# The order of the steps on VectorE, ScalarE, SP and GpSimd in a two-layer adapter kernel

## The chip, the cores and the metric

The kernel runs on one core of a Trainium2 chip. The metric is the device time of one execution in microseconds (us). All matrix products run on TensorE; the other engines (VectorE, ScalarE, GpSimd) and the DMA queue that SyncE (SP) issues have their own instruction streams and meet only at semaphores.

## The reference

Two layers of the same form follow each other. Each of 128 items has a role out of three (its row of weights), and the roles drawn are only two of them, so a layer sorted by role has one change of weights in it.

```python
h = einsum('bsh,bhk->bsk', x, W_down[role]) + b_down[role]     # x: (128, 128, 1024), K = 512
h = gelu(h, approximate=False)
u = einsum('bsk,bkh->bsh', h, W_up[role]) + b_up[role]
y = x + u
x = (y - mean(y)) * rsqrt(var(y) + 1e-5) * gamma[role] + beta[role]
```

## The kernel before

**Pairs and steps.** The items are sorted by role and taken two at a time: 65 pairs in a layer, 130 pairs `p` in all (layer 0 is pairs 0 to 64, layer 1 is 65 to 129). `e` is 0 or 1, the item within a pair. Every engine runs one function `step(i)` (or `begin(i)` and `end(i)`) for a rising pair number `i`, and works in it on several pairs at once: `i` goes down, `w = i-2` is split for the up product, `u = i-3` goes up and is added to its rows, `u-1 = i-4` (for GpSimd and SP `z`) is normalised and stored. In layer 1 the rows come from `mid`, where layer 0 stored them.

**TensorE.** Matrices are multiplied as three products of high and low parts (high x high, high x low, low x high) in full-width matmuls of 512 columns. A step i has 90 of them, in blocks of six: `product(u, 0)`, `down(i, 0, 0)`, `product(u, 1)`, `down(i, 0, 1)`, `product(u, 2)`, `down(i, 0, 2)`, `product(u, 3)`, `down(i, 0, 3)`, `product(u, 4)`, `down(i, 1, 0)`, `product(u, 5)`, `down(i, 1, 1)`, `product(u, 6)`, `down(i, 1, 2)`, `down(i, 1, 3)`. The up product is done by a scheme of seven products instead of eight (Winograd's form), whose sums of blocks of h are made by GpSimd (`sums`) and whose sums of weights by VectorE (`factors`). Steps 0 to 2 have no products, steps 130 to 132 have no `down`. The products 0, 2, 4, 6 go to the bank `bX`, the products 1, 3, 5 to `bZ`, where some stay to be added to. Product 2 waits for `onto` 1 to have read its bank, product 3 for `onto` 2, product 4 for `onto` 3, product 5 for `last_onto` 4, product 6 for `last_onto` 5 (all by the count `s_v`).

**What TensorE waits for besides.** `down(i, 0, 0)` needs `xl`, the low part of x (VectorE's `low_x(i, 0)`, after ScalarE's `high_x(i, 0)`), the bias in its bank (`seed_d`), and an increase of `s_wd[0]` by VectorE's `ready(i, s_wd[0])`, which comes in every step whether weights are new or not. `s_wd[1]` stands before `down(i, 0, 2)`. The products wait in the same way for `s_wu[0]` (products 0 and 1), `s_wu[1]` (2 and 3) and `s_wu[2]` (4 to 6), and for `low_h` 0 to 3, the low parts of h and its sums: product 0 for the first, products 1 and 2 for the second, product 3 for the third, product 5 for the fourth.

**VectorE** runs `end(i-1)` and then `begin(i)` as one body. Its `low_*` and `take_*` functions subtract high parts; `transpose_h` and, in layer 1, `transpose_x` transpose what DMAs laid out in blocks; `onto` and `last_onto` add a bank to the rows (the evictions; the last of them also sum the row), `mean`, `variance` and `scale` (rows minus mean, times gamma) belong to the normalisation. **ScalarE** rounds to the high parts (`high_*`, `take_*`), does `gelu`, writes biases into banks (`seed_*`), squares and `normal` (times 1/sigma), and issues the loads of new weights (`load_up`, `load_down`, 2 MB each). **GpSimd** does `sums`, two small steps of `norm` and `shift` (plus beta), and increases `s_cg`, for which `scale` waits. **SP** issues all other DMAs: `store_h` writes gelu's result to `htok` in DRAM, `load_h` fetches it back in blocks once it has landed, `load_blocks` fetches x in blocks (`xq`, for the down product), `load_rows` fetches x in rows, `store` writes rows out.

**Order and queues.** The order within a step is written out by hand, and each engine takes its instructions in that order. `kinds.when_new(p, do)` is an `If` on a register: it runs `do` only where pair p has other weights than the pair before. That is so for pairs 30, 65 and 95, so that new down weights are taken for steps 30, 65 and 95, and their new up weights are first used in steps 33, 68 and 98 (`w` is such a pair in steps 32, 67 and 97). `when_far` runs loads and `factors` for the same pairs; `when_near` never finds a pair here.

**Loops.** `steps` and `plain_steps` unroll six steps into the body of a hardware loop. VectorE's jumps back lie between `begin` and the following `end`, in layer 0 before `end(9)`, `end(15)` and so on (steps 10, 16, ... 58 of TensorE), in layer 1 before `end(74)`, ... `end(122)` (steps 75, 81, ... 123):

```python
def body(i):
    end(i + -1)
    begin(i)
```

## Time and profile before

| | us |
|---|---|
| median of 3 runs | 2741.23 (2740.98 to 2743.66) |
| profiled execution, its own time | 2742.87 |
| its span, first to last instruction | 2741.1 |
| TensorE busy | 2682.4 (98%) |
| VectorE busy | 2200.2 (80%) |
| ScalarE busy | 1668.7 (61%) |
| GpSimd busy | 1375.2 (50%) |

PE is TensorE, PEld its weight loads, DVE VectorE, ACT ScalarE, POOL GpSimd, SP SyncE; an engine with a q is its queue, which issues DMAs and increases semaphores. The busy time of an engine is the union of its rows; matmul rows overlap. In a timeline a row is the start in us from the span's start, its length in us, the engine, the source line, the operation, what it writes and reads, how many alike were merged, and in brackets how long the engine stood idle before it and what ended that. L537 is a matmul of `down`, L549 of `product`, L888 `low_wd`, L907 `low_wu`, L913 to L917 `factors`, L926 the last step of `take_wu_0`, L959 `ready`, L968 `transpose_x`, L975 `low_x`, L982 `transpose_h`, L997 `low_h`, L1007 `onto`, L1015 `last_onto`, L1023 `mean`, L1038 `scale`, L661 `high_x`; L287 is the load of up weights, L334 `load_blocks` in layer 1, L381 `store_h`, L389 `load_h`, L311 the load of up biases.

### The profile page before, as it was taken

To read this page: it belongs to the slowest core of one execution; us is meant where nothing else is said; L and a number is where in the kernel's file an instruction comes from. 1 tells how busy PE (TensorE), PEld (TensorE's weight loads), DVE (VectorE), ACT (ScalarE), POOL (GpSimd) and SP (SyncE) were. 2 spreads that over 40 slices of the span, in tenths; PEclk is the share of its full clock that TensorE was granted. 3 is DMA by queue.
4 is the path that set the end of the run, shared out by engine and by line. 5 is a ranking of instruction groups with operands and counts; after the bars stand their busy time and mean duration, and the time that the engine had idled before them with its cause. 6 is when DMAs were issued, how large, how long until landed. Compare 5 with 4: busy or idle time off the path is not lost.

```text
span 2741.1 us, 54380 instructions
## 1 busy us (share of the span) xinstructions
PE 2682.4 (98%) x11720; PEld 2200.6 (80%) x11720; DVE 2200.2 (80%) x3360; ACT 1668.7 (61%) x2906; POOL 1375.2 (50%) x1050
## 2 busy tenths in 40 slices
PE   8999999998999999999989999999989999999996
PEld 6888888887888888888778888888768888888885
DVE  6777777779777777777898888888888888888886
ACT  5656656666656665666656665665656565665664
POOL 1455455555545555555444454554445455545545
PEclk9999999999999999999999999999999999999999
DMA  6656566566666656656766566666766666666664
GB/s 221 219 198 219 200 209 211 202 233 223 222 205 204 209 205 209 212 201 225 235 200 220 187 222 203 206 214 201 242 197 214 199 223 191 222 204 203 214 193 149
DMA packets 360737, 573.36 MB, mean 209 GB/s; under 512 B 40162, under 2 KB 239970, under 8 KB 359394
## 3 DMA queue, kind: packets, MB, share of 16 engines
q1 hardware_dynamic: 358850, 554.14, 61.5%
q10 hardware_dynamic: 1440, 15.47, 1.6%
q14 instruction: 435, 3.56, 0.4%
q8 instruction: 12, 0.20, 0.0%
HBM read 364.97 MB, written 204.47 MB: 208 GB/s over the span
## 4 chain that ended last, share of the span: by engine, by line
PE 87%; DVE 6%; issue 5%; ACT 1%; DMA 1%; POOL 1%; DVEq 1%; ACTq 0%; POOLq 0%; SPq 0%
PE pD L537 46%; PE bX L549 23%; PE bZ L549 18%; DVE wul L907 1%; DVE xt L1015 1%; DVE hl L997 1%; DVE xT L968 0%; DVE xt L1007 0%; DMA rwu<-in_Wu 0%; DVE xt L1038 0%; DVE hT L982 0%; DVE xl L975 0%; DVE wdl L888 0%; POOL cs L486 0%; POOL cs L488 0%
## 5 line engine op out<-in xcount | busy, mean ns | idle before, releaser
L537 PE MATMUL pD<-wdh,xh 128*128 128x512 f32 x2080 | 811.6, 390 | 13.7 <-DVEq L959 10.1
L478 POOL TENSOR_TENSOR xt<-xt,cgb 128x1024 f32<-128x1024 f32 x258 | 630.1, 2443 | 364.8 <-ACT xt L729 364.8
L537 PE MATMUL pD<-wdh,xl 128*128 128x512 f32 x2080 | 810.4, 390 | 0.0
L537 PE MATMUL pD<-wdl,xh 128*128 128x512 f32 x2080 | 810.1, 389 | 0.0
L486 POOL TENSOR_TENSOR cs<-hT 128x256 f32<-128x256 f32 x130 | 150.7, 1159 | 910.6 <-DVE hT L982 910.6
L721 ACT ACTIVATE pC<-xt,nmean 128x512 f32<-128x512 f32 x520 | 359.8, 692 | 257.7 <-DVE nmean L1023 248.9
L729 ACT ACTIVATE xt<-xt,rstd 128x1024 f32<-128x1024 f32 x258 | 297.1, 1152 | 307.4 <-POOL rstd L471 303.9
L537 PEld LDWEIGHTS pD<-wdh,xh 128*128 128x128 f32 x2080 | 391.0, 188 | 100.3 <-DVEq L959 13.3
L537 PEld LDWEIGHTS pD<-wdh,xl 128*128 128x128 f32 x2080 | 391.0, 188 | 81.6
L537 PEld LDWEIGHTS pD<-wdl,xh 128*128 128x128 f32 x2080 | 391.1, 188 | 80.8
L549 PE MATMUL bX<-wuh,hh 128*128 128x512 f32 x1040 | 406.8, 391 | 18.2 <-DVE xt L1007 10.5
L549 PE MATMUL bX<-wul,hh 128*128 128x512 f32 x1040 | 405.1, 390 | 0.0
L549 PE MATMUL bX<-wuh,hl 128*128 128x512 f32 x1040 | 405.0, 389 | 0.0
L997 DVE TENSOR_TENSOR hl<-cs,hh 128x512 fp32r<-128x512 f32 x260 | 302.0, 1180 | 112.1 <-issue 105.7
L711 ACT ACTIVATE hh<-cs 128x512 fp32r<-128x512 f32 x260 | 163.9, 630 | 359.4 <-PE bX L549 240.5
L1038 DVE SCALAR_TENSOR_TENSOR xt<-xt,nmean,cgb 128x1024 f32<-128x1024 f32 x260 | 327.3, 1299 | 10.3 <-POOLq L499 6.7
L549 PE MATMUL bZ<-wuh,hh 128*128 128x512 f32 x780 | 307.4, 394 | 13.3 <-issue 7.6
L549 PE MATMUL bZ<-wul,hh 128*128 128x512 f32 x780 | 304.9, 391 | 0.0
L549 PE MATMUL bZ<-wuh,hl 128*128 128x512 f32 x780 | 304.8, 391 | 0.0
L1007 DVE TENSOR_TENSOR xt<-bX,xt 128x512 f32<-128x512 f32 x260 | 178.7, 687 | 129.8 <-PE bX L549 129.0
L549 PEld LDWEIGHTS bX<-wuh,hh 128*128 128x128 f32 x1040 | 195.3, 188 | 65.4 <-DVE xt L1007 15.0
L1015 DVE SCALAR_TENSOR_TENSOR xt<-bX,xt 128x512 f32<-128x512 f32 x260 | 177.1, 681 | 88.1 <-PE bX L549 88.0
(119 smaller groups left out, 3830.5 us busy)
## 6 DMA issues: line engine op xcount, KB each, us to landing
xq<-in_xB SPq DMA_DIRECT2D x130, 512.0 KB, 3.6
htok<-hg SPq DMA_DIRECT2D x260, 256.0 KB, 2.9
hq<-htok SPq DMA_DIRECT2D x1040, 64.0 KB, 2.2
xt<-in_x SPq DMA_DIRECT2D x130, 512.0 KB, 4.2
mid<-xt SPq DMA_DIRECT2D x130, 512.0 KB, 3.7
xq<-mid SPq DMA_DIRECT2D x520, 128.0 KB, 3.1
xt<-mid SPq DMA_DIRECT2D x130, 512.0 KB, 4.6
out<-xt SPq DMA_DIRECT2D x128, 512.0 KB, 3.0
```

What stands on the lines that cost most here:

```text
L478: eng.tensor_tensor(xt[:, k, :], xt[:, k, :], cgb[:, 1, :], ALU.add).then_inc(s_o, 1)
L486: eng.tensor_tensor(cs[:, 0, :], b1, b2, ALU.add).then_inc(s_S, 1)
L537: last = eng.matmul(pD[e][:, :], a[:, e, 128 * k:128 * k + 128], w[:, k, :], start=False, stop=(k == 7 and n == 2), skip_group_check=True)
L549: last = eng.matmul(bank[:, :], a[:, left, 128 * c:128 * c + 128], w[:, n, c, :], start=(start and c == 0 and m == 0), stop=(c == 1 and m ...
L711: eng.activation(dst, src, ACT.Copy).then_inc(s_hh, 1)
L721: eng.activation(junk[:, :], xt[:, u.slot(e), K * m:K * m + K], ACT.Square, bias=nmean[:, n:n + 1], accum_out=ssq[:, b, m, e:e + 1]).then_ ...
L729: eng.activation(xt[:, k, :], xt[:, k, :], ACT.Copy, scale=rstd[:, n:n + 1]).then_inc(s_z, 1)
L907: eng.tensor_tensor(wul[:, n, :, :], block, wuh[:, n, :, :].bitcast(fp32), ALU.subtract)\
L997: eng.tensor_tensor(blocks, src, high.bitcast(fp32), ALU.subtract).then_inc(s_hl, 1)
L1007: eng.tensor_tensor(half(u, e, m), bank[:, :], half(u, e, m), ALU.add).then_inc(s_v, 1)
L1015: eng.scalar_tensor_tensor(out=half(u, e, m), in0=bank[:, :], scalar=1.0, in1=half(u, e, m), op0=ALU.mult, op1=ALU.add, accum_out=ys[:, b, ...
L1038: eng.scalar_tensor_tensor(out=xt[:, k, :], in0=xt[:, k, :], scalar=nmean[:, n:n + 1], in1=cgb[:, 0, :], op0=ALU.add, op1=ALU.mult).then_i ...
```

## The change

Steps are put in another order on four engines, and nothing else is changed: no instruction is added or removed, and every wait stays with its step. On VectorE the evictions and the later parts of a step change places with the work on new weights (`take_*`, `factors`), one of the two `scale` goes behind `last_onto` 4, `low_h` 0 goes behind it too, `transpose_x(i+1, 1)` and `last_onto` 7 go to the head of `end`, and `ready(i+1, s_wd[0])` stands behind them. On ScalarE `gelu(i, 0)` goes ahead of `high_x(i+1, 0)`, `high_h` 0 ahead of `gelu(i-1, 1)`, and the loads of weights are spread over `end`. On SP `load_blocks(i+1, 1)` goes behind `load_h(v, 1)`, both stores go ahead of `store_h(i, 0)` and `load_blocks(i+2, 0)`, and the loads of biases and gains go from the end into the middle. On GpSimd `sums` goes behind the increase of `s_cg` and the wait for new gains.

```diff
--- before.py
+++ after.py
@@ -411,21 +411,21 @@
                 kinds.read(i + 1)
                 load_h(v, 0)
                 store_h(v, 1)
+                load_rows(w, 0)
+                load_h(v, 1)
                 if not (i + 1).first():
                     load_blocks(i + 1, 1)
-                load_h(v, 1)
-                load_rows(w, 0)
-                load_rows(w, 1)
-                store(z, 0)
-                store_h(i, 0)
-                if not (i + 1).first():
-                    load_blocks(i + 2, 0)
-                store(z, 1)
-                kinds.when_new(u, gains)
                 if i.first():
                     up_biases(i)
                 if not v.first():
                     kinds.when_new(v, up_biases)
+                kinds.when_new(u, gains)
+                load_rows(w, 1)
+                store(z, 0)
+                store(z, 1)
+                store_h(i, 0)
+                if not (i + 1).first():
+                    load_blocks(i + 2, 0)
 
             steps(eng, step, -1, NPH + 4, 2, 6, 5)
             for k in range(4):
@@ -492,11 +492,11 @@
 
             def step(i):
                 w, z = i + -2, i + -4
-                sums(w)
                 if z.exists():
                     kinds.read(z)
                     kinds.when_new(z, take_gb)
                     eng.sem_inc(s_cg, 1)
+                sums(w)
                 norm(z)
                 shift(z, 0)
                 shift(z, 1)
@@ -747,49 +747,49 @@
                 kinds.read(i + 2)
                 if not i.first():
                     high_x(i, 1)
-                gelu(i + -1, 1)
-                if not i.first():
-                    seed_d(i, 1)
                 if (i + -2).first():
                     take_wu_2(Pair(0))
-                high_h(i + -2, 0)
                 if i.first():
                     fetch_up(eng, adapter(i), 0)
                 if not (i + -3).first():
                     kinds.when_new(i + -3, take_wu_2)
+                high_h(i + -2, 0)
+                gelu(i + -1, 1)
+                if not i.first():
+                    seed_d(i, 1)
 
             def end(i):
                 u, w = i + -3, i + -2
                 if not (i + 1).first():
                     kinds.when_new(i + 1, load_bias)
+                high_h(w, 1)
                 kinds.when_near(w, load_up)
+                normal(u + -1, 0)
                 kinds.when_far(i, load_up)
+                gelu(i, 0)
                 kinds.when_near(i + 1, load_down)
-                kinds.when_far(i + 2, load_down)
-                high_h(w, 1)
                 if not w.first():
                     kinds.when_new(w, take_wu_0)
-                normal(u + -1, 0)
                 if not (i + 1).first():
                     high_x(i + 1, 0)
-                gelu(i, 0)
-                high_h(w, 2)
+                if (i + -1).first():
+                    take_wu_0(Pair(0))
+                kinds.when_far(i + 2, load_down)
+                seed_x(w)
+                normal(u + -1, 1)
                 if not (i + 1).first():
                     seed_d(i + 1, 0)
-                normal(u + -1, 1)
                 if not (i + 1).first():
                     kinds.when_new(i + 1, take_wd_0)
-                seed_x(w)
+                high_h(w, 2)
+                square(u, 0, 0)
                 seed_z(w)
-                square(u, 0, 0)
+                high_h(w, 3)
                 square(u, 0, 1)
-                high_h(w, 3)
+                square(u, 1, 0)
                 if not (i + 1).first():
                     kinds.when_new(i + 1, take_wd_1)
-                square(u, 1, 0)
                 square(u, 1, 1)
-                if (i + -1).first():
-                    take_wu_0(Pair(0))
 
             steps(eng, halves(begin, end), -1, NPH + 5, 0, 5, 5)
 
@@ -1072,44 +1072,44 @@
                     last_rows(u + -1)
                     return
                 onto(u, 1, X, 0, 0)
+                transpose_h(w, 0)
                 if not i.first():
                     kinds.when_new(i, take_wd_1)
-                ready(i, s_wd[1])
                 if u.first():
                     take_wu_6(Pair(0))
-                transpose_h(w, 0)
+                ready(i, s_wd[1])
                 transpose_h(w, 1)
+                onto(u, 2, bZ, 1, 1)
+                if u.last():
+                    variance(u + -1)
                 if not i.first():
                     low_x(i, 1)
+                onto(u, 3, X, 0, 1)
                 if (i + -1).first():
                     factors(Pair(0))
                 if (i + -2).first():
                     take_wu_1(Pair(0))
+                if not u.last():
+                    variance(u + -1)
                 kinds.read(i + 1)
-                onto(u, 2, bZ, 1, 1)
-                low_h(w, 0)
-                if u.last():
-                    variance(u + -1)
-                onto(u, 3, X, 0, 1)
                 if not u.first():
                     kinds.when_new(u, take_wu_2)
                 ready(u, s_wu[2])
+                scale(u + -1, 0)
+                last_onto(u, 4, bZ, 0, 1, 3)
                 kinds.when_near(w, factors)
-                if not u.last():
-                    variance(u + -1)
+                low_h(w, 0)
                 if only_up(i):
                     low_h(w, 1)
-                scale(u + -1, 0)
                 scale(u + -1, 1)
-                last_onto(u, 4, bZ, 0, 1, 3)
                 transpose_x(i + 1, 0)
                 last_onto(u, 5, X, 1, 1, 2)
                 if not w.first():
                     kinds.when_new(w, take_wu_0)
                     ready(w, s_cb)
-                ready(w, s_wu[0])
                 if not (i + 1).first():
                     low_x(i + 1, 0)
+                ready(w, s_wu[0])
                 last_onto(u, 6, bZ, 0, 0, 1)
                 mean(u, 0, 6)
 
@@ -1117,21 +1117,20 @@
                 u, w = i + -3, i + -2
                 if (u + -1).last():
                     return
+                transpose_x(i + 1, 1)
+                last_onto(u, 7, bX[u.c % 2], 1, 0, None)
                 if not (i + 1).first():
                     kinds.when_new(i + 1, take_wd_0)
                 ready(i + 1, s_wd[0])
-
-                if not only_up(i):
-                    low_h(w, 1)
-                transpose_x(i + 1, 1)
-                low_h(w, 2)
                 if w.first():
                     take_wu_4(Pair(0))
-                last_onto(u, 7, bX[u.c % 2], 1, 0, None)
-                mean(u, 1, 7)
                 kinds.when_far(i + -1, factors)
                 if not w.first():
                     kinds.when_new(w, take_wu_1)
+                if not only_up(i):
+                    low_h(w, 1)
+                mean(u, 1, 7)
+                low_h(w, 2)
                 ready(w, s_wu[1])
                 low_h(w, 3)
                 if (i + -1).first():
```

## Rows read from the trace of the kernel before

**Rows 1.** The page, part 1: busy us (share) xinstructions of each engine

```profile
PE 2682.4 (98%) x11720; PEld 2200.6 (80%) x11720; DVE 2200.2 (80%) x3360; ACT 1668.7 (61%) x2906; POOL 1375.2 (50%) x1050
```

**Rows 2.** The chain of waits: start us, us, what; 26 such pieces, first two

```profile
70.33 2.72 PE pD L537 x12
...
90.73 2.72 PE pD L537 x12
```

**Rows 3.** TensorE by stretches: us, busy (matmuls), granted clock, DMA share, GB/s

```profile
590.00:720.00 130.00, 121.25 (x523) 0.99 0.67 223
...
1930.00:2070.00 140.00, 128.03 (x542) 0.99 0.71 224
...
2690.00:2741.10 51.10, 30.44 (x119) 0.90 0.39 140
```

**Rows 4.** Timeline of TensorE, step 75

```profile
1547.06 0.39 PE L549 MATMUL bX<-wuh,hh 128*128 128x512 f32 x1
...
1555.30 0.50 PE L549 MATMUL bZ<-wuh,hh 128*128 128x512 f32 x1
...
1567.71 0.39 PE L549 MATMUL bX<-wuh,hh 128*128 128x512 f32 x1
```

**Rows 5.** Timeline of VectorE around two jumps of its loop

```profile
318.57 1.30 DVE L997 TENSOR_TENSOR hl<-cs,hh 128x512 fp32r<-128x512 f32 x2 [5.17 <-issue]
...
1542.55 0.21 DVE L1023 TENSOR_SCALAR nmean<-ys 128x1 f32<-128x1 f32 x1
...
1547.22 0.69 DVE L997 TENSOR_TENSOR hl<-cs,hh 128x512 fp32r<-128x512 f32 x1 [4.45 <-issue]
...
1549.58 0.67 DVE L1015 SCALAR_TENSOR_TENSOR xt<-bX,xt 128x512 f32<-128x512 f32 x1
```

**Rows 6.** Timeline of ScalarE, step 74

```profile
1538.73 1.03 ACT L661 ACTIVATE xh<-xT 128x1024 fp32r<-128x1024 f32 x1 [0.57 <-DVE xT L968]
```

**Rows 7.** Timelines of VectorE and TensorE at the first layer's new up weights

```profile
645.97 1.22 DVE L913 TENSOR_TENSOR rwu<-rwu 128x1024 f32<-128x1024 f32 x1
...
660.18 4.57 DVE L907 TENSOR_TENSOR wul<-rwu,wuh 128x1024 fp32r<-128x1024 f32 x2
...
664.67 3.42 DVE L926 TENSOR_TENSOR rwu<-twu,rwu 128x1024 f32<-128x1024 f32 x1
...
670.23 0.50 PE L537 MATMUL pD<-wdh,xh 128*128 128x512 f32 x1 [2.31 <-DVEq L959]
...
676.85 0.50 PE L549 MATMUL bX<-wuh,hh 128*128 128x512 f32 x1 [2.22 <-DVE xt L1007]
...
680.56 2.90 DVE L907 TENSOR_TENSOR wul<-rwu,wuh 128x1024 fp32r<-128x1024 f32 x2
...
685.43 0.47 PE L549 MATMUL bX<-wuh,hh 128*128 128x512 f32 x1 [2.64 <-DVEq L959]
```

**Rows 8.** Timeline of TensorE at the last new down weights

```profile
1968.74 0.50 PE L549 MATMUL bZ<-wuh,hh 128*128 128x512 f32 x1 [1.61 <-DVE xt L1007]
```

**Rows 9.** Timelines of VectorE and TensorE in step 131

```profile
2710.73 2.47 DVE L1038 SCALAR_TENSOR_TENSOR xt<-xt,nmean,cgb 128x1024 f32<-128x1024 f32 x2
...
2713.91 0.75 PE L549 MATMUL bZ<-wuh,hh 128*128 128x512 f32 x1 [3.17 <-issue]
```

**Rows 10.** Timelines of ScalarE's, SP's queues and VectorE, step 95

```profile
1968.13 0.35 ACTq L287 DMA_DIRECT2D rwu<-in_Wu  x1
...
1969.04 2.33 SPq L334 DMA_DIRECT2D xq<-mid  x4
...
1976.81 1.74 SPq L389 DMA_DIRECT2D hq<-htok  x4
...
1979.03 1.26 DVE L968 STREAM_TRANSPOSE xT<-xq 128x1024 f32<-128x1024 f32 x1 [0.50 <-DMA xq<-mid]
```

**Rows 11.** Timelines of SP and ScalarE near the start

```profile
27.50 0.34 SPq L311 DMA_DIRECT2D cbu<-in_bu  x1
...
35.44 1.06 ACT L661 ACTIVATE xh<-xq 128x1024 fp32r<-128x1024 f32 x1 [7.04 <-DMA xq<-in_xB]
```


## The prediction

> **What bounds the kernel now.** I read the page first. TensorE is busy for 98% of the span [rows 1], so every other engine counts only where TensorE waits for it. The chain of waits then gives the pace: the same twelve matmuls come back every 20.40 us [rows 2], one step of 90 matmuls, 0.227 us each. 11,700 matmuls at that pace are 2652 us of the 2741.1 us span. The other 89 us are what an order of steps can touch: a start of some 13 us before the first real matmul, some 11 us after the last, and about 65 us of pauses. Third, TensorE by stretches [rows 3] shows where these are: 8.8 us idle at the change of weights in the first layer, 12.0 at the change in the second, and 20.7 in the last 51 us; the second layer's first weights have their share too. A pause costs some 0.16 us more than its idle time, because a matmul's row is 0.39 long and the pace 0.227, and more where the clock dips (0.90 at the end [rows 3]). The ordinary steps are at the floor: there an earlier operation gains nothing, and only a later one can matter.
>
> **Where the limits lie within a step.** Count from the first matmul of product 0. `down(i,0,0)` starts at 1.36, product 1 at 2.72, product 2 at 5.44, product 3 at 8.16, product 5 at 13.6, product 6 at 16.3 (blocks of six matmuls, 1.36 each). Product n's bank is readable some 0.15 us after its end, so `last_onto` 7 can start at 17.85.
>
> **Ordinary steps.** Walking the new order through with the durations of rows, VectorE's `scale`, 1.24 us each [rows 9], now has one copy before `last_onto` 4 and one after, with `low_h` 0 (0.4) between them. `ready(s_wd[0])`, which releases `down(i+1,0,0)`, is moved from before `low_h` 1 to behind `transpose_x(i+1,1)` and `last_onto` 7. In an ordinary step of layer 1 that is about 18.75, against 21.76 when it is wanted; `low_h` 1 ends near 19.6, wanted at 23.1. ScalarE's `high_h` 2 goes from 13.5 to about 17, and its use is at 28. SP stores both halves before `store_h(i,0)`: it goes from 14.8 to about 19.5, and what it feeds is used a step later. All hidden: cost 0, with 2 to 3 us of cover. If the cover were gone the price would be that of the next part.
>
> **The jump at the end of VectorE's loop body.** VectorE's code is a loop of six steps, and at each jump it stands still: 4.45 us [rows 5], with no releaser but "issue", always right after `mean(u,0)` and before the first operation of `end` (5.17 in the longest, in layer 0). In layer 1 `mean` starts at 15.9 of the step before (1542.55 less 1526.66), so the first operation runs at 1547.22, and TensorE's step began at 1547.06 [rows 4]. `ready` is now the first thing after the jump, just in time. In the new order it stands behind a 1.25 us transposition and `last_onto` 7 (0.69).
> There is also a delay ahead of the jump. In layer 1 `transpose_x(i+1,0)` now comes after `low_h` 0 and a second `scale`: it ends near 13.4 instead of 12.0. ScalarE's `high_x`, which waits for it already [rows 6], ends at 14.6; `low_x` and `last_onto` 6 follow, and `mean` starts near 16.5, 0.6 later. Then 4.4 for the jump, 1.16 and 0.69: `ready` at 22.9 to 23.1 against 21.76, so TensorE pauses for 1.2 us, with the restart 1.35. From this the kernel before has its own loss at these steps to be taken off: product 3 starts late there (1555.30) and the step is 20.65 long, 0.25 too much [rows 4]; eight such steps have lost 1.7 in all. The new order has `onto` 2 ahead of `low_x(i,1)` and ends that. Eight jumps: 8 x 1.35 - 1.7 = **+9.1**. Bounds: 0.9 each if the skipped `If`, now behind the jump's cover, saves 0.25 (+5.5), and 1.8 each if the wait grows (+12.7).
> In layer 0 there is no transposition, and `mean` is not later. `ready` comes 0.8 after the jump ends; it passes if the jump ends before 0.5 of the step. It ended at 0.88 in the worst [rows 5], so one or two pauses: **+0.5** (0 to 2).
> The Trainium skill ("Runtime: NRT & Kernel Launch", Instruction fetch mechanics) says that a taken branch to code outside the fetched window stalls until it is fetched. The trace agrees at the loop's jump (4.45 us), while skipped `If` blocks cost 0.25 to 0.5. If the rule struck the skipped blocks too, the new places of the `If`s right behind the jump would be worse than I count.
>
> **New up weights (three times).** Now VectorE runs `take_wu_0` (4.57 for two `wul`, 3.42 for `b11` [rows 7], stretched because GpSimd runs at the same time) ahead of `low_x`, and TensorE waits 2.31; then `take_wu_1` makes `onto` 1 late, 2.22; then `take_wu_2` with product 4, 2.64. In the new order: `factors` (three at 1.22) ahead of `low_h` 1 makes product 1 late by 0.4 in the step before; `last_onto` 4, `scale` and the others are earlier, so `ready(s_wd[0])` is about 0.4 late in layer 0 and 1.7 in layer 1 (two transpositions more); `take_wu_1`, now ahead of `low_h` 1, delays product 1 by 1.9 to 2.2; `take_wu_2` ahead of `scale` and `last_onto` 4 still holds product 4 back, by 1.9 to 2.0. So 5.0 for 7.2 in layer 0, and 6.1 for about 8.4 in layer 1.
> **New down weights (three times).** `take_wd_1` and `low_x(i,1)` stood before `onto` 2, and product 3 waited 1.61 [rows 8]; with `onto` 2 ahead of `low_x` (1.2) some 0.3 to 0.5 is left. That is 1.3 less in layer 0, 2.1 at the layer's start and 3.6 at the last change.
> **Blocks behind a load of weights.** This goes against the change. SP's `load_blocks(i+1,1)` moves behind `load_h(v,1)` and `load_rows`, and VectorE's `transpose_x(i+1,1)` moves ahead of `last_onto` 7. At the last change the 2 MB of up weights were issued at 1968.13, the blocks at 1969.04, and the transposition found them only at 1979.03, 10.9 after the weights' issue; nothing urgent stood behind it [rows 10]. Now `last_onto` 7 and `ready` do: blocks at 22.5, `ready` at 24.5, a pause of 2.7 us, at both layer-1 loads. Once, in step 94, SP's own loop jump and the load of down weights coincide; blocks near 22, then `take_wd_0`, `ready` at 26.4, a pause of 4.6. The landing of `htok`, for which `load_h(v,1)` waits, took 8 us there (1968.48 to 1976.81 by the second of these issues). Together 10 us, bounds 0 (blocks issued before the weights) and 14.
> Sums with the restarts: layer 0 **-4.5**; the layer's start -5.5 + 3.0 = **-2.5**; the last change, before it 17.8 of pauses, after it 0.5 + 6.1 with restarts (8.4), a jump 1.35, blocks 3.0 and 4.6: **0**.
>
> **The end.** In the last steps, without `down`, product 5 waits for `last_onto` 4, which stands behind two `scale` (2.47 together) and these behind GpSimd's `sums`, because `s_cg` is increased after `sums`: 3.17 of pause [rows 9], and much the same a step earlier. Now `s_cg` is first, and one `scale` is behind. I get product 5 earlier by 3.3, 4.4 and 4.4 in the three steps, but part is lost again, because `low_h` 2 waits for GpSimd's `shift`: last matmul earlier by **-4** (-1 to -6).
> **The start.** `gelu(0,0)` (0.58) goes ahead of `high_x(1,0)`, and `cbu`'s load, now at 27.50, is issued before the blocks for which ScalarE waited 7.04 us [rows 11]; `ready(s_wd[1])` follows a transposition: **+1** (0 to +3).
> GpSimd's `take_gb` ahead of `sums`, `gains` ahead of `load_rows(w,1)`: both are hidden, by some 2 us, three times; if not, up to +3.
>
> **Sum:** -4.5 - 2.5 + 0 - 4 + 1 + 9.1 + 0.5 = -1.4 to the profiled execution (2742.87, with 1.8 around its span). The median is 2741.23; half a microsecond of the small unknowns above is kept for a loss: 2740.3.
>
> **Rivals.**
> A, the sum: gains at the weights and the end, eaten by the loop jumps. Chance 0.43. 2735.8 to 2746.7.
> B, the gains win: blocks land in time (10 less) or the jump's pauses are 0.9 (3.6 less). For it: SP's issues at the first change of layer 1 came close to the transposition's time anyway (the wait was only 0.50). Against it: the order is fixed and the transposition's place moves forward by itself. 2727 to 2735, 2730 if blocks alone are in time. Chance 0.33.
> C, slower: blocks are late not only near weights. In the step behind each SP loop jump I get the blocks' landing at 19.3 and the transposition from 19.5, `ready` at 21.45 against 21.76. It decides from a landing after 19.7: each microsecond is paid eight times, so 1 us late is +8, 2749; with the longer jump pauses 2752. Chance 0.24.
> D, nothing moves: VectorE would have to run 1.3 us ahead at the jumps and stay as late at weights. It is within A's band; the rows with 4.45 speak against it.
> The skill's page "SBUF — State Buffer" (Who interferes with whom) has the lock between VectorE and GpSimd held for a whole instruction. `b11`, 3.42 long in place of 1.22, agrees; moved operations may meet GpSimd elsewhere, which would be spread over B and C.
>
> **Numbers.** A measurement here tells 0.2%, 5.5 us, from no change. Faster 0.33, same 0.43, slower 0.24. The range reaches into B and C, 2729 to 2750; A's own is 2736 to 2746.
>
> **What would show it.** After VectorE's jump in layer 1: transposition, `last_onto` 7, and TensorE paused by 1.0 to 1.5 us before `down(i,0,0)`, released by `ready`; steps of 21.7 there. Product 3 never late at jumps. Pauses at product 1, no longer at `onto` 1, at new up weights. In steps 66 and 96 the transposition waiting for the blocks. Last matmul 4 us sooner. It is wrong if `mean(u,0)` isn't later in layer 1, if blocks land before 16.7, or if ordinary steps aren't 20.40.

## The result, and the profile after

| | before | after |
|---|---|---|
| median of 19 runs each | 2742.59 (2740.98 to 2746.26) | 2747.16 (2743.09 to 2755.03) |
| ratio, 95% interval | | 1.0016 [1.0010, 1.0023] |
| profiled execution, its span | 2742.87, 2741.1 | 2747.39, 2745.5 |

The change costs some 4.6 us. That is inside the band of 0.2% and inside the range (2729 to 2750), but the forecast had its sign the other way (2740.3, 0.9 under the 2741.23 that it started from). The page, part 1, and TensorE by stretches (us, busy with matmuls, granted clock, DMA share, GB/s), which answer to [rows 1, 3]:

```profile
PE 2684.8 (98%) x11720; PEld 2202.1 (80%) x11720; DVE 2158.2 (79%) x3360; ACT 1680.4 (61%) x2906; POOL 1318.5 (48%) x1050
```

```profile
590.00:720.00 130.00, 126.11 (x539) 0.97 0.65 220
1930.00:2070.00 140.00, 127.04 (x537) 0.95 0.65 210
2690.00:2745.50 55.50, 35.22 (x142) 0.92 0.39 143
```

The first stretch has gained, the second has lost, and the ordinary pace of 20.40 is unchanged. To see every pause, each gap from one matmul's start to the next is taken, less the pace of 0.2267 us, and summed by stretch. All kernels run later stand in the same table, since it is what tells them apart ("start" is up to 80 us, "first" 600 to 720, "layer 1" 1310 to 1445, "last" 1925 to 2125, "end" from 2660; "rest" is the ordinary steps and the jumps; "jumps" is the length of the steps behind VectorE's jumps in layer 1, without the one in the last change of weights). All in us:

```
                           start first layer1 last  end rest  all | jumps        | median  ratio to before, 95%
before                      6.6  11.8  14.0  17.4 13.3  1.7  64.9 | 20.40-20.73  | 2742.59
after                      11.6   8.3   9.7  23.4 11.6  3.7  68.2 | 20.40-21.42  | 2747.16 1.0016 [1.0010, 1.0023]
forecast of the change     +1    -4.5  -2.5   0   -4   +9.6  -0.4 | 21.7         |
measured change            +5.0  -3.5  -4.3  +6.0 -1.7 +2.0  +3.4
```

The other microsecond of the 4.4 between the two spans lies behind the last matmul. The pauses themselves, in TensorE's timeline:

```profile
42.19 0.76 PE L537 MATMUL pD<-wdh,xh 128*128 128x512 f32 x1 [5.03 <-ACT pD L680]
51.94 0.47 PE L537 MATMUL pD<-wdh,xh 128*128 128x512 f32 x1 [1.71 <-ACT pD L680]
675.88 0.79 PE L549 MATMUL bZ<-wuh,hh 128*128 128x512 f32 x1 [2.66 <-DVE hl L997]
687.91 0.47 PE L549 MATMUL bX<-wuh,hh 128*128 128x512 f32 x1 [0.69 <-DVEq L959]
1400.59 0.50 PE L549 MATMUL bZ<-wuh,hh 128*128 128x512 f32 x1 [1.93 <-DVE hl L997]
1964.35 0.79 PE L537 MATMUL pD<-wdh,xh 128*128 128x512 f32 x1 [8.59 <-DVEq L959]
2716.16 0.47 PE L549 MATMUL bZ<-wuh,hh 128*128 128x512 f32 x1 [0.54 <-issue]
2722.80 0.47 PE L549 MATMUL bZ<-wuh,hh 128*128 128x512 f32 x1 [0.93 <-DVE hl L997]
2725.93 0.50 PE L549 MATMUL bX<-wuh,hh 128*128 128x512 f32 x1 [1.50 <-DVE xt L1007]
```

Where [rows 7] had 2.31, 2.22 and 2.64 there are now 2.66 at product 1 and 0.69 at product 4. One pause of 8.59 at the last new down weights is larger than everything gained there. In the end [rows 9] product 5's 3.17 is 0.54, but `low_h` and `onto` have 0.93 and 1.50 in its place, and product 6 has 1.09.

A pause has a second price behind it. TensorE by stretches, the 8.59 and what follows it:

```profile
1955.00:1964.30 9.30, 0.76 (x4) 0.69 0.59 197
1964.30:1968.70 4.40, 4.35 (x10) 0.50 0.91 298
1968.70:1975.00 6.30, 6.30 (x29) 0.99 0.55 177
```

After the idle stretch the granted clock is 0.50, the lower of its two levels (1.2 GHz), for ten matmuls, which start 0.43 us apart instead of 0.23. That adds 2.2 us to the 8.59, and it is part of the 23.4 in the table.

**What is behind the 8.59.** The chain of waits of the kernel after, around it, is told almost only by SP's queue:

```profile
1930.87 9.99 DMA out<-xt
...
1941.69 0.33 SPq L381
...
1944.63 3.48 issue
...
1950.79 2.84 DMA htok<-hg
...
1957.18 2.81 DMA xq<-mid
1960.02 0.06 DVE xT L968
...
1961.87 2.28 DVE wdl L888 x2
```

In layer 1 `store(z, 1)` waits until the first store has landed. While the 2 MB of down weights (issued at 1928.90) come in, that takes 9.99 us. Before, `store_h(i, 0)` was issued ahead of this wait, at 1934.28; now it stands behind it, at 1941.69. The 3.48 of "issue" is SP standing still at its own loop jump, as it did for 2.9 before. `load_h(v, 1)` has its own landing to wait for (2.84), and `load_blocks(i+1, 1)` stands behind that, at 1955.65, 21.8 us into step 94; before it was issued at 13.0 of the step. VectorE's transposition waits for the blocks, and `last_onto` 7, `take_wd_0` and `ready` stand behind the transposition:

```profile
1960.02 1.26 DVE L968 STREAM_TRANSPOSE xT<-xq 128x1024 f32<-128x1024 f32 x1 [7.74 <-DMA xq<-mid]
```

This is not the only place. The transposition finds its blocks late again in steps 99 to 101 (2.34, 3.69 and 5.92), and TensorE pauses six times there, by 3.6 us together, where the kernel before had one pause of 0.91. With SP's old order (`e5`, below) none of these is left. Which wait of SP makes them was not looked for.

**The jumps.** In layer 1 there are two kinds of steps. Times are from the start of the step (1646.42 for step 80, 1768.82 for step 86). In four of the eight, as step 80, VectorE's second `scale` starts 0.09 us ahead of GpSimd's first `shift` and takes 1.28; `mean(u, 0)` is at 16.09, and the next step is 20.40 long. In the other four, as step 86, it starts 0.03 to 0.16 behind the `shift` and takes 3.43; `mean` is at 18.23, and the next step is 21.2 to 21.4. VectorE's and GpSimd's timelines, steps 80 and 86:

```profile
1657.10 1.28 DVE L1038 SCALAR_TENSOR_TENSOR xt<-xt,nmean,cgb 128x1024 f32<-128x1024 f32 x1
1657.19 3.45 POOL L478 TENSOR_TENSOR xt<-xt,cgb 128x1024 f32<-128x1024 f32 x1 [1.27 <-ACT xt L729]
...
1665.70 1.26 DVE L968 STREAM_TRANSPOSE xT<-xq 128x1024 f32<-128x1024 f32 x1 [2.98 <-issue]
...
1779.34 2.50 POOL L478 TENSOR_TENSOR xt<-xt,cgb 128x1024 f32<-128x1024 f32 x1 [1.27 <-ACT xt L729]
1779.50 3.43 DVE L1038 SCALAR_TENSOR_TENSOR xt<-xt,nmean,cgb 128x1024 f32<-128x1024 f32 x1
...
1790.29 1.26 DVE L968 STREAM_TRANSPOSE xT<-xq 128x1024 f32<-128x1024 f32 x1 [3.03 <-issue]
```

Whoever comes second waits until the other is done. The second `scale` starts at 10.67 to 10.68 of the step in all eight; it is the `shift` that moves (10.52 to 10.78). It follows the first `scale` by 2.6 us: in step 80, beside the later first `scale`, GpSimd's last step of `norm` takes 0.88 instead of 0.63, and ScalarE's `normal` and the `shift` stand behind it. The first `scale` starts at 7.91 or at up to 8.17, according to how long VectorE's register load of `kinds.read(i+1)` just ahead of it takes. That load in step 80 and in step 86 (ns, smallest, median and largest of one):

```profile
L248 DVEq TENSOR_LOAD <-c_kind x1: 546/546/546, 1653.5 to 1653.5; - x1
L248 DVEq TENSOR_LOAD <-c_kind x1: 300/300/300, 1775.9 to 1775.9; - x1
```

In the steps ahead of the eight jumps the load takes 0.54 to 0.57 where the second `scale` is short and 0.30 to 0.42 where it is long. So a slower register load lets VectorE come first. What makes the load slow was not tried.

The idle time at the jump itself is 2.84 to 3.05 in seven of the eight, where [rows 5] had 4.45.

### The profile page after: what moved, and what is told of

Its sections match the earlier page's. It is cut to its first block, busy times and chain, and to the rows that moved or that the text cites. A ratio compares the mean times of both kernels' runs of the same rounds, so it can differ in the third digit from the quotient of the medians.

```text
span 2745.5 us, 54419 instructions
## 1 busy us (share of the span) xinstructions
PE 2684.8 (98%) x11720; PEld 2202.1 (80%) x11720; DVE 2158.2 (79%) x3360; ACT 1680.4 (61%) x2906; POOL 1318.5 (48%) x1050
## 4 chain that ended last, share of the span: by engine, by line
PE 83%; DVE 5%; issue 4%; DMA 3%; SPq 2%; POOL 1%; ACT 1%; DVEq 0%; ACTq 0%; POOLq 0%
PE pD L537 44%; PE bX L549 22%; PE bZ L549 17%; DMA htok<-hg 1%; DMA out<-xt 1%; DVE xt L1038 1%; DVE wul L907 1%; POOL xt L478 1%; DVE xt L1015 1%; SPq L389 1%; DVE hl L997 1%; DMA xq<-mid 0%; DVE wdl L888 0%; SPq L334 0%; DVE xT L968 0%
## 5 line engine op out<-in xcount | busy, mean ns | idle before, releaser
L478 POOL TENSOR_TENSOR xt<-xt,cgb 128x1024 f32<-128x1024 f32 x258 | 676.8, 2624 | 523.4 <-ACT xt L729 523.4
L1038 DVE SCALAR_TENSOR_TENSOR xt<-xt,nmean,cgb 128x1024 f32<-128x1024 f32 x260 | 499.0, 1919 | 25.7 <-issue 23.4
L486 POOL TENSOR_TENSOR cs<-hT 128x256 f32<-128x256 f32 x130 | 96.4, 741 | 797.8 <-DVE hT L982 775.5
L549 PE MATMUL bZ<-wuh,hh 128*128 128x512 f32 x780 | 307.4, 394 | 16.5 <-DVE hl L997 13.6
L661 ACT ACTIVATE xh<-xT 128x1024 fp32r<-128x1024 f32 x130 | 133.0, 1023 | 166.1 <-DVE xT L968 155.7
```

Of the source, the lines that this page charges most:

```text
L478: eng.tensor_tensor(xt[:, k, :], xt[:, k, :], cgb[:, 1, :], ALU.add).then_inc(s_o, 1)
L486: eng.tensor_tensor(cs[:, 0, :], b1, b2, ALU.add).then_inc(s_S, 1)
L549: last = eng.matmul(bank[:, :], a[:, left, 128 * c:128 * c + 128], w[:, n, c, :], start=(start and c == 0 and m == 0), stop=(c == 1 and m ...
L661: eng.activation(xh[:, e, :], src, ACT.Copy).then_inc(s_xh, 1)
L1038: eng.scalar_tensor_tensor(out=xt[:, k, :], in0=xt[:, k, :], scalar=nmean[:, n:n + 1], in1=cgb[:, 0, :], op0=ALU.add, op1=ALU.mult).then_i ...
```

## The experiments

In every table row below the columns are those of the table above; "before" ran beside each at 2741 to 2743.

### Which engine's order costs

`e4_vector_alone`: before, with VectorE's new order only. `e5_sp_before`: after, with SP's old order. `e12_gpsimd_before`: the same with GpSimd's old order too. Their edits are whole blocks of the diff.

> The kernel before, with VectorE's new order alone. Theory (gains are VectorE's, losses are ScalarE's at the start and SP's at the second layer's new down weights): no wait for seed_d at the start (the start's pauses at most 7 us in all), the pause of 8.59 at most 4, and the whole 3 to 7 us faster than before (0.998 to 0.9985). Rival (VectorE's order pays only with the others', or is itself what costs): no faster than before.

> The kernel after, with SP's whole order from the kernel before. Theory (SP's order makes the two largest pauses: load_blocks(i+1, 1) behind load_h and behind a store that waits for another's landing): the pause at the second layer's new down weights, 8.59 us in after and 4.51 with the second store late, falls under 1 us, and the first steps lose 3 us less (after: about 11.6 in the first 60 us). The pauses at VectorE's jumps grow by up to 0.5 us each, since the kernel with SP's and the others' old order has idle times of 3.5 there in place of 2.9. Together 6 to 9 us faster than after: 0.998 to 1.0 of before. Rival (the late blocks come from VectorE's and ScalarE's later steps): the pause stays above 3 us.

> The kernel after with the old order of SP (2730.11 with that alone) and of GpSimd: only VectorE and ScalarE in the new order. Theory: at the end VectorE's first scale waits for the count that GpSimd increases behind sums, product 5 waits for last_onto 4 behind that scale, and GpSimd's part of the change is what took it away: the end's pauses go from 11.4 us back towards 13.3, and the time is 2 us more, 2732; the steps after VectorE's jumps keep their 0.9 to 1.1. Rival: GpSimd's order gives nothing (with VectorE's order alone the end had 10.4): 2729 to 2730, and the end 10.4.

```
                           start first layer1 last  end rest  all | jumps        | median  ratio to before, 95%
e4_vector_alone             3.3   8.6  15.0  17.6 10.4 11.7  66.6 | 21.8-22.1    | 2745.67 1.0015 [1.0006, 1.0025]
e5_sp_before                7.2   6.8   8.7  10.9 11.6  8.0  53.1 | 21.3-21.5    | 2730.11 0.9952 [0.9936, 0.9967]
e12_gpsimd_before           8.0   6.7   8.7  11.5 10.3  7.6  52.8 | 21.3-21.6    | 2727.73 0.9945 [0.9932, 0.9959]
```

SP's order alone costs 15 us of pauses (68.2 less 53.1); without it the change would have been a gain of 12 us. VectorE's order alone, expected to be 3 to 7 us faster than before, is 3.5 slower: it gains nothing at the start of layer 1 (15.0), where ScalarE's is needed with it (8.7 in `e12`), and its jumps cost 11.7. GpSimd's order is worth nothing; at the end its old one is 1.3 better.

### Which part of SP's order

```diff
 e10_blocks_ahead:                        e2_second_store_late:
+if not (i + 1).first():                   store(z, 0)
+    load_blocks(i + 1, 1)                -store(z, 1)
 load_rows(w, 0)                           store_h(i, 0)
 load_h(v, 1)                              if not (i + 1).first():
-if not (i + 1).first():                       load_blocks(i + 2, 0)
-    load_blocks(i + 1, 1)                +store(z, 1)
```

`e11_blocks_and_store` has both.

> The kernel after, with SP's store(z, 1) again behind store_h(i, 0) and load_blocks(i+2, 0). Theory (the second store, which waits for the first one's landing, holds up everything behind it while 2 MB of down weights are loaded, 10.6 us for the two stores): the pause of 8.59 us at the second layer's new down weights shrinks to 5 to 6.5, the whole is 2 to 3.5 us faster than after. Rival (the place of load_blocks(i+1, 1) behind load_h and load_rows alone makes it): the pause stays over 7.5.

> The kernel after, with SP's load_blocks(i+1, 1) back ahead of load_rows(w, 0) and load_h(v, 1); everything else of SP stays in the new order. SP's whole old order took the 8.59 us pause at the last new down weights down to 1.3 us and won 15 us; the old place of store(z, 1) alone took it to 4.51. Theory: what is left is the place of the blocks, which now stand behind the wait for htok's landing; with them ahead the pause is 4 to 5 us, the start's pauses fall from 11.6 to 7 or 8 (the blocks are what ScalarE waits for there), and the time is 6 to 9 us under the kernel after: 2737 to 2740. Rival: the store that waits for its landing in front of the blocks decides alone; then the place changes under 2 us at the last weights, and only the start moves: 2742 to 2745.

> The kernel after, with both of SP's places put back: load_blocks(i+1, 1) ahead of load_rows and load_h(v, 1), and store(z, 1) last. Theory: these two are all that counts in SP's order, and the time is that of SP's whole old order, 2730 to 2732, with the last new down weights' pause at 1 to 1.5 us. Rival: the loads of biases and gains in the middle, and load_rows(w, 0) ahead, cost something of their own: 2735 or more, with pauses at the start above 7.2 us.

```
                           start first layer1 last  end rest  all | jumps        | median  ratio to before, 95%
e2_second_store_late       11.2   7.2   9.5  14.7 11.6  8.9  63.1 | 21.3-21.8    | 2742.94 1.0006 [0.9996, 1.0015]
e10_blocks_ahead            7.1   7.2  10.2  12.5 11.6  3.5  52.1 | 20.40-21.3   | 2733.17 0.9969 [0.9958, 0.9980]
e11_blocks_and_store        7.2   7.0   7.8   9.9 11.6  8.2  51.7 | 21.2-21.5    | 2733.88 0.9968 [0.9956, 0.9980]
```

The place of one load decides: `e10` wins 16.1 of pauses, 10.9 at the last change and 4.5 at the start, more than expected. SP's queue, VectorE and TensorE in it:

```profile
1941.26 1.74 SPq L389 DMA_DIRECT2D hq<-htok  x4
...
1943.90 1.85 SPq L334 DMA_DIRECT2D xq<-mid  x4
...
1949.15 1.26 DVE L968 STREAM_TRANSPOSE xT<-xq 128x1024 f32<-128x1024 f32 x1 [2.15 <-DMA xq<-mid]
...
1953.48 0.50 PE L537 MATMUL pD<-wdh,xh 128*128 128x512 f32 x1 [3.00 <-DVEq L959]
```

The first store's landing is still waited for (8.71 in its chain), and SP's jump takes 4.9 here, but the blocks are issued at 15.3 of the step instead of 21.8, and the pause is 3.00 instead of 8.59. Moving only the store gets it down to 4.51. With both, 1.02. What `e11` wins at the weights it loses at the jumps, where all eight steps are of the later kind, so the two edits together are no better than the first. It is the place of `store(z, 1)` that does this: all eight are of the later kind in `e2` too, and the register load takes 0.30 to 0.31 ahead of each of its jumps.

### The start

`e1_first_weights_late`: after, with ScalarE's rounding for the first pair back at the end.

```diff
-                if (i + -1).first():
-                    take_wu_0(Pair(0))
                 kinds.when_far(i + 2, load_down)
...
                 square(u, 1, 1)
+                if (i + -1).first():
+                    take_wu_0(Pair(0))
```

`e9_first_pair` does this on `e5_sp_before`, and puts `take_wu_2(Pair(0))` back behind `seed_d(i, 1)`.

> The kernel after, with ScalarE's take_wu_0 for the first pair of all back at the end of its step instead of ahead of seed_d. Theory (ScalarE's order at the start): the waits of TensorE for seed_d (5.03 and 1.71 us near 42 and 52 us) come from the 4.1 us of weight rounding put ahead of seed_d; the first goes, the matmul at 42.19 starts near 39.8, the whole is 2 to 4 us faster than after (about 0.1% below it). Rival (DMA): the start is late because htok's landing and the blocks are queued behind 2.5 MB of weights and biases; then that matmul moves by less than 1 us.

> The kernel after with SP's order of before (2730.11 in its own run), and on ScalarE the roundings of the first pair's up weights (the one in begin and the one in end) put back to where they were before. Theory: at the start ScalarE's early roundings make seed_d late by themselves; SP's old order brought the start's pauses from 11.6 to 7.2 us, and with ScalarE's old places the rest to before's 6.6 or to the 3.4 that VectorE's order alone had, so 1 to 4 us fewer: 2726 to 2729, ratio 0.994. Rival: they only move, as in the run that did this without SP's order (5.03 went and 6.01 came, one step later): 2730 to 2731.

```
                           start first layer1 last  end rest  all | jumps        | median  ratio to before, 95%
e1_first_weights_late      12.0   7.3   9.8  22.6 11.6  3.9  67.1 | 20.40-21.4   | 2750.00 1.0029 [1.0019, 1.0039]
e9_first_pair               4.0   6.8   8.1   9.7 11.6  8.0  48.2 | 21.3-21.5    | 2728.76 0.9950 [0.9937, 0.9964]
```

In `e1` the 5.03 goes and 6.01 comes one step later; the first theory fell. ScalarE shows why:

```profile
44.80 1.06 ACT L661 ACTIVATE xh<-xq 128x1024 fp32r<-128x1024 f32 x1 [4.18 <-DMA xq<-in_xB]
...
49.52 0.60 ACT L680 ACTIVATE pD<-cbd 128x512 f32<-128x512 f32 x1
```

It waits for blocks that SP issued late, and the roundings stand between that wait and the bias. Two causes in a row: taking SP's away gives 4.4 (`e5`), and then ScalarE's another 3.2 (`e9`).

### The jumps: first attempts

`e3_if_ahead`: `take_wd_0` and `ready` ahead of the transposition in `end`. `e6_scales_together`: both `scale` ahead of `last_onto` 4. `e7_transposition_late`: `transpose_x(i+1, 1)` behind `low_h` 1. `e8_combined`: `e6`, `e7`, SP's old order and ScalarE's two roundings at their old places.

```diff
 e3_if_ahead:
+if not (i + 1).first():
+    kinds.when_new(i + 1, take_wd_0)
+ready(i + 1, s_wd[0])
 transpose_x(i + 1, 1)
 last_onto(u, 7, bX[u.c % 2], 1, 0, None)
```

> The kernel after, with VectorE's If for take_wd_0 and ready(s_wd[0]) back at the head of end, ahead of transpose_x and last_onto 7. Theory (the first skipped If right behind the loop's jump costs 1.5 us of its own, and work ahead of it hides that): VectorE's idle time at its jumps goes from 2.9 back to about 4.4 us, TensorE gets pauses of 0.3 to 1.5 us for low_h 1 or last_onto at about nine steps in layer 1, 3 to 9 us slower than after. Rival (the jump costs 2.9 us now because its fetch begins earlier or is shorter with this code layout): idle stays near 2.9 and the time within 2 us of after. At the second layer's new down weights both expect a pause of about 7 in place of 8.6, since low_h 1 still stands behind the late transposition.

> The kernel after, with both scales ahead of last_onto 4 again. Theory (the second scale now meets GpSimd's first shift and takes 3.43 us instead of 1.28, mean is 2.1 us later, 18.2 instead of 16.1 in the step, and this alone makes the pauses after VectorE's jumps in layer 1): every scale 1.24 to 1.3 us, mean at 16.1 in every ordinary step, steps after jumps 20.40 to 20.6 in all nine cases (after: 21.2 to 21.4 in four of eight), 3 to 4 us faster than after; the end loses up to 2 us, as last_onto 4 is later there. Rival (the transposition's place at the head of end alone makes them): steps after jumps stay at 21 or more.

> The kernel after, with VectorE's transpose_x(i+1, 1) moved behind ready(s_wd[0]) and low_h 1. Theory (what makes late blocks cost TensorE time is that ready and low_h 1 stand behind the transposition that waits for them): the pause of 8.59 us at the second layer's new down weights falls to under 3 us though the blocks are as late as before, and the steps after jumps are 20.40 to 20.7. 6 to 9 us faster than after. Rival (the blocks' lateness reaches TensorE anyway, through mean, low_h 2 and high_x): the pause only moves, 6 us or more in the two steps together.

> The kernel after, with SP's old order, both scales ahead of last_onto 4, the transposition behind low_h 1, and ScalarE's two roundings of the very first up weights (take_wu_0 and take_wu_2 for pair 0) back behind seed_d. Theory (the new order's gains are at the new up weights and the end, its losses are these four places): about 6 us of pauses left in the first 60 us, 8 and 9 at the first two changes of weights, 9 at the last, 12 at the end, nothing at the jumps: 45 to 50 in all against 65 before and 68 after, 10 to 18 us faster than before (0.9935 to 0.9965). Rival (the gains at the weights need the very order that makes the losses): 5 us faster at most.

```
                           start first layer1 last  end rest  all | jumps        | median  ratio to before, 95%
e3_if_ahead                12.8   6.9  12.5  23.5 11.6  5.8  73.0 | 20.40-21.9   | 2748.88 1.0031 [1.0018, 1.0043]
e6_scales_together         12.6  14.0   9.6  22.1 12.4  0.9  71.4 | 20.4-20.6    | 2754.60 1.0038 [1.0025, 1.0051]
e7_transposition_late      10.2   7.2  12.4  20.1 11.6  3.1  64.6 | 20.40-20.9   | 2746.16 1.0013 [1.0004, 1.0022]
e8_combined                 4.2  12.8  11.1  12.5 12.4  0.6  53.5 | 20.40-20.7   | 2731.91 0.9959 [0.9946, 0.9973]
```

`e3`: the jump's idle time grows from 2.9 to 3.24 to 3.9 in layer 1, not to 4.4, so the `If` behind the jump is only a part of the 1.5 us. `e6` (3 to 4 us faster than after was expected, 7.4 slower came): the jumps' pauses go, but 5.7 us come at the first change, where a step is already long and the loop jumps in it. VectorE's idle time at that jump is 5.80 instead of 2.91 (why is not known), and TensorE pauses behind it:

```profile
704.50 0.80 PE L537 MATMUL pD<-wdh,xh 128*128 128x512 f32 x1 [4.45 <-DVEq L959]
```

`e7` (6 to 9 us faster than after was expected, 1.0 came): the 8.59, which stands in TensorE's step 95, becomes 1.14, 1.47 and 1.36 in step 95 and 4.09 in step 96: a late landing is paid wherever its first reader stands. `e8` is no better than `e5`, because it trades the jumps (8.0 to 0.6) for the first change (6.8 to 12.8).

### Who comes first, scale or shift

`e13_scale_first` puts the second `scale` 0.34 us earlier (10.34 of the step instead of 10.68); `e16_low_ahead` instead takes `low_h` out from between:

```diff
 e13_scale_first:                         e16_low_ahead:
 scale(u + -1, 0)                         scale(u + -1, 0)
 last_onto(u, 4, bZ, 0, 1, 3)            +low_h(w, 0)
+scale(u + -1, 1)                         last_onto(u, 4, bZ, 0, 1, 3)
 kinds.when_near(w, factors)              kinds.when_near(w, factors)
 low_h(w, 0)                             -low_h(w, 0)
 ...                                      ...
-scale(u + -1, 1)                         scale(u + -1, 1)
```

`e14` and `e17` are the same two edits on `e9_first_pair`, `e15` and `e18` on it with GpSimd's old order as well.

> The kernel after, with scale(u-1, 1) straight behind last_onto 4 and low_h(w, 0) behind that scale. Theory: in the kernel after the second scale starts at 10.68 us of the step and GpSimd's first shift at 10.52 or 10.77; the one that comes second waits for the other, so the scale takes 1.28 or 3.43. Started at 10.3 it always comes first: 1.28 in every step of layer 1, mean at 16.1, no step of 21.2 to 21.4 behind a jump, and 3.5 us less than the kernel after: 2743.5. In layer 0, where the scale starts 0.26 behind the shift, it comes first too. Rival: the 3.43 isn't set by who comes first, and the scale is as long as before wherever it is put: mean at 18.2 in some steps, time within 1 us of the kernel after.

> SP's order of before, ScalarE's two first-pair roundings at their old places (2728.76 so far), and the second scale straight behind last_onto 4. Theory: all eight jumps of layer 1 had the mean at 18.23 and cost 0.9 to 1.05 each, and four or more pauses of 0.3 at product 1; with the scale of 1.28 they go: 7 to 8 us less, 2721. Rival: the jump's idle time grows as the mean comes earlier (it was 3.6 to 4.1 in layer 0 with SP's old order, where the mean is at 16.57, and 2.9 to 3.1 in layer 1 at 18.23), so the first transposition starts at 20.4 instead of 21.4 and ready is at 22.3, still 0.6 late: 2724 to 2726.

> As the run before, with GpSimd's order of before as well. Theory: GpSimd's order has no part in the race, and at the end its old order was worth 1.3 us (pauses of 10.3 in place of 11.6): 1 us less than the run before. Rival: with sums ahead of the count that the first scale waits for, that scale starts later, the shift too, and the margin of the second scale changes: some scales of 3.43 come back, 1 us each.

> The kernel after, with low_h(w, 0) moved ahead of last_onto 4, between the first scale and it. Theory: an operation of VectorE with two SBUF inputs that comes second to GpSimd's shift waits for its end, and the next of its kind inherits the wait. Here low_h runs at 9.4, before any shift, last_onto 4 (one input in PSUM, never delayed so far) at 9.9, and the second scale at 10.4 to 10.5, ahead of the shift at 10.5 to 10.8; behind it come a transposition and an eviction, which don't wait. So the scale takes 1.28 in every step, mean is at 16.1 in all of layer 1, the four steps of 21.2 to 21.4 go, and the time is 3 to 4 us under the kernel after: 2743.5. Rival: last_onto 4 becomes late by 0.15 and the scale with it, the race stays open as it is: 2747, with scales of both lengths.

> SP's order of before, ScalarE's two first-pair roundings at their old places (2728.76), and low_h(w, 0) ahead of last_onto 4. Theory: the eight jumps of layer 1 lose their 0.9 to 1.05 and the 0.3 at product 1 behind each: 7 to 8 us less, 2721. Rival: with SP's old order the jump's idle time was 3.6 to 4.2 where the mean was early (layer 0), so in layer 1 the first transposition starts at 20.3 and ready is at 22.2, still 0.5 late: 2724 to 2725.

> As the run before, with GpSimd's order of before as well. Theory: its order plays no part in the race in ordinary steps, because the first scale starts where variance lets it, and at the end its old order is worth 1.3 us: 1 us less than the run before. Rival: no difference within 1 us either way.

```
                           start first layer1 last  end rest  all | jumps        | median  ratio to before, 95%
e13_scale_first            11.7  15.8  10.6  26.7 10.0 18.9  93.7 | 21.3-21.5    | 2770.31 1.0100 [1.0085, 1.0116]
e14_first_pair_scale_first  4.3  13.7   7.9  15.5 10.0 40.6  92.0 | 21.4-21.9    | 2766.54 1.0082 [1.0068, 1.0096]
e15_gpsimd_before_too       3.1  11.9   9.8  14.1 11.4 37.1  87.3 | 21.4-21.8    | 2769.27 1.0100 [1.0085, 1.0116]
e16_low_ahead              10.4   7.3   9.1  22.4 10.6  0.0  59.8 | 20.40        | 2740.41 0.9997 [0.9988, 1.0006]
e17_first_pair_low_ahead    5.4   7.1   7.9   8.3 10.6  0.0  39.3 | 20.40        | 2716.84 0.9907 [0.9892, 0.9922]
e18_gpsimd_low_ahead        4.9   6.6   7.9   8.4 10.4  0.0  38.1 | 20.40        | 2716.17 0.9905 [0.9890, 0.9920]
```

`e13` missed by 27 us and `e14` by 45, and the miss is the best proof. The `scale` does take 1.28 in every step, as expected. But the next operation with two SBUF inputs inherits the wait (step 80, which starts at 1665.30):

```profile
1675.63 1.28 DVE L1038 SCALAR_TENSOR_TENSOR xt<-xt,nmean,cgb 128x1024 f32<-128x1024 f32 x1
1676.09 3.07 POOL L478 TENSOR_TENSOR xt<-xt,cgb 128x1024 f32<-128x1024 f32 x1 [1.27 <-ACT xt L729]
1676.83 2.62 DVE L997 TENSOR_TENSOR hl<-hT,hh 128x256 fp32r<-128x256 f32 x1
1679.37 1.25 DVE L968 STREAM_TRANSPOSE xT<-xq 128x1024 f32<-128x1024 f32 x1
```

`low_h` takes 2.62 where it took 0.42, so that no step of layer 1 is of the early kind any more, and layer 0's `low_x` comes later and meets the second `shift` (3.31 where it was 2.26). Each of the sixteen jumps outside the changes of weights now costs 0.9 to 1.1, and on SP's old order (`e14`) seven of the eight in layer 0 cost 3.9 to 4.1 and one 2.3. `e6` had the same: its `low_h` took 2.28. In `e16` only a transposition and an eviction from PSUM follow the `scale`. These two don't wait for GpSimd: in all twenty traces `transpose_x` never took over 1.26 us and an eviction never over 0.69. Every `mean` ahead of these jumps is at 15.89, every step behind one is 20.40 long, and the rest's pauses are 0.0. `e17` adds SP's and ScalarE's repairs and is 0.93% under before. VectorE's `scale` in it (count, busy us, mean ns):

```profile
L1038 DVE SCALAR_TENSOR_TENSOR xt<-xt,nmean,cgb 128x1024 f32<-128x1024 f32 x260 | 344.8, 1326 | 26.7 <-issue 22.1 <-POOLq L498 2.0 <-DVE wul L907 1.0
```

In the kernel after the same row is:

```profile
L1038 DVE SCALAR_TENSOR_TENSOR xt<-xt,nmean,cgb 128x1024 f32<-128x1024 f32 x260 | 499.0, 1919 | 25.7 <-issue 23.4
```

## Why the prediction was right or wrong

- **The sum itself:** the parts as written give -0.4, not -1.4 (-4.5 - 2.5 + 0 - 4 + 1 + 9.1 + 0.5). By the prediction's own last step the forecast would have been 2741.3, which is no change. So the forecast of a small gain rested on a slip of 1.0. The terms of layer 0 and of the layer's start add up to 3.5 and 4.4 before "restarts"; the working doesn't show the other microsecond of each.
- **Ordinary steps, cost 0:** right. They are 20.40 in every kernel, with the `scale` at 3.43 too, as long as no jump follows.
- **Loop jumps, +9.1 and +0.5, measured +2.0 together:** mis-sized by 7.6, by two errors of opposite sign. The mean was put at 16.5 and the jump at 4.4. The jump took 2.9. The mean is at 16.09 in four steps, which then have room, and at 18.23 in four, because the `scale` was priced at 1.24 [rows 9] without its meeting with the `shift`. Those four pay 0.8 to 1.0 each. The sentence that moved operations may meet GpSimd elsewhere named the mechanism and gave it no price and no place. The other four have room only because VectorE's register load is slow there (0.54 to 0.57), which no row of the kernel before showed. The Trainium skill ("SBUF — State Buffer", Who interferes with whom) says that an instruction of VectorE with two SBUF inputs contends with one of GpSimd that reads SBUF, and that issue order decides who waits. The runs agree: 1.28 against 3.43, 0.42 against 2.62, and no wait for the evictions.
- **New up weights and layer 0, -4.5, and layer 1's start, -2.5:** right in kind; measured -3.5 and -4.3. Pauses sit at product 1 and no longer at `onto` 1. The 3.0 for blocks behind the up weights' load did not come, which is most of the difference at the layer's start: ScalarE issues that load behind the blocks of that time, at 1346.29 behind 1343.45, and at the last change at 1977.68 behind 1975.10.
- **The last change, 0, measured +6.0:** this is the step that failed most. The pause behind VectorE's step 94 was forecast at 4.6 and was 8.59, and the lower clock behind it cost 2.2 more, where a restart was priced at 0.16, "and more where the clock dips". Late blocks in steps 99 to 101 had no term and cost some 2.7 more than before. The forecast had the waits for `htok` and the blocks, not the store that stands ahead of `store_h` and waits for its neighbour's landing, which the load of weights stretches to 9.99. "`store_h(i,0)` ... what it feeds is used a step later" was called hidden; the wait put ahead of it was the head of this chain. `e10` (3.00), `e2` (4.51) and `e11` (1.02) show both parts.
- **The end, -4, measured -1.7:** the 3.17 went as forecast, and more of it than expected came back at `low_h` and `onto`, so the term was 2.3 too large. That GpSimd's order does it is wrong: with its old order the end is shorter (10.3).
- **The start, +1 (0 to +3), measured +5.0:** outside its bounds, and the second step that failed. The load of blocks had been counted as issued behind `cbu` only; it also stands behind `load_h(v, 1)` (42.68), and ScalarE's roundings of the first up weights, which had no term at all, follow it. `e5` and `e9` show 4.4 and 3.2 for the two.
- **Rivals:** A, the sum, came nearest, 0.5 above its own range (2747.16 against 2746.7), and that is luck: the jumps were 7.6 too dear, the last change 6.0, the start 4.0 and the end 2.3 too cheap. C's place, blocks late in the step behind each SP jump, was wrong: they were late where weights came in. B's terms were real: with the blocks in time (`e10`) the time is 2733, and with SP's old order, ScalarE's roundings late and `low_h` moved (`e17`) it is 2717.
- **Signs named:** product 3 is no longer late at jumps, and pauses moved from `onto` 1 to product 1, as said. The steps behind jumps are 21.2 to 21.4 in four cases, not 21.7 in all. The transposition waited for late blocks behind step 94 and in 99 to 101, not in 66 and 96. The end has 1.7 us less of pauses, not 4. `mean(u, 0)` is later in layer 1, by 0.2 in four steps and by 2.3 in four, where 0.6 was named.

**Still open:** why VectorE's jump takes 2.9 in one order and 3.6 to 4.5 in another. An `If` directly behind it adds 0.3 to 0.9 (`e3`). With an early mean in layer 1 it is 3.6 to 4.2 on SP's old order (`e17`) and 2.9 to 3.1 on its new one (`e16`). In layer 0 the place of `store(z, 1)` alone brings it from 2.7 to 3.0 up to 3.7 to 4.3 (`e2`), and that of the blocks does not (`e10`, 2.8 to 3.1). But on SP's old order, with the mean at 15.89 in both, it is 2.9 to 3.1 in layer 0 of `e17` and 3.9 to 5.1 in that of `e8`, so SP's order is not the whole of it. The cause is not shown, and neither is what stretches the register load.

## What to carry to other kernels

When a step is moved on a DMA queue, list every wait that it carries, such as for another transfer's landing, and read how long that landing takes while the largest load is in flight; then see what is queued behind it. When operations of VectorE and GpSimd overlap, price each two-SBUF-input operation at both lengths, and look at the next one too: an operation moved out of the way hands the wait on. In these traces only evictions and transpositions filled the window for free, and one position of one 0.42 us operation was worth 7 us here (`e16`) and 12 us on the repaired order (`e17`).

## What was not expected of the hardware

- A race of 0.03 to 0.16 us between two engines decides over 2.15 us of one operation, and which way it falls changes from step to step of one run and with SP's order: the `scale` is late in four of eight in the kernel after, in all eight with SP's old order. It goes by whether one register load of VectorE takes 0.3 or 0.55 us.
- The stall at a taken loop jump is no constant: 2.7 to 5.9 us on VectorE in these kernels (5.94 at the first change in `e13`).
- A store of 512 KB that lands in 3.2 us (median of the page) takes 7.4 (before), 8.7 (`e10`) and 10.0 us (after) behind a load of 2 MB.
